# Who writes the causal mask of the scores: TensorE by identity products, or ScalarE by a copy into the score banks

## The chip, the cores and the metric

One Trainium2 chip, one of its cores. The metric is device time in microseconds for one execution of the whole program, lower is better. In the engine names below PE is TensorE (PEld its weight loads), DVE is VectorE, ACT is ScalarE, POOL is GpSimd, SP the engine that only issues transfers here.

## The reference: one decoder layer on 16 sequences of 128 tokens

Three residual blocks, each behind a layer norm: an RWKV-like attention with a decay matrix, a causal attention to a context, and a mixture of 8 experts plus a shared one. The change touches the second block alone:

```python
qp = q @ Wq.T
kv = latent_kv @ Wkv_expand.T
k, v = jnp.split(kv, 2, axis=-1)
...
scores = jnp.einsum('bhqd,bhkd->bhqk', qh, kh) * inv_sqrt_d      # 16 heads of 16
causal = jnp.tril(jnp.ones((sq, sk), dtype=bool))
scores = jnp.where(causal, scores, jnp.finfo(scores.dtype).min)
attn = jax.nn.softmax(scores, axis=-1)
out = jnp.einsum('bhqk,bhkd->bhqd', attn, vh)
```

## The kernel before

**Groups and batches.** The 16 sequences go in four groups of four (`g` = 0 to 3; `GB` = 4 sequences a group, called batches, `b` = 0 to 3). A group passes through the first attention (scores, decay, products), a normalisation and projection stage (points `n0` to `n5`), the causal attention (the x stage, points `x0a` to `x3c`), and the norm, mixed inputs and routing of the third block (`y0`, `r0`, `r1`). The mixture itself, called the feed-forward, of group g-1 is woven into group g in ticks: each engine has its own program, written out by hand in the same order, and at a `point(g, name)` it runs the ticks that stand there. From g = 1 on, a batch of the x stage holds five ticks: two at `a`, one at `b`, two at `c`. The last group's ticks run alone behind it. Order is by program order on each engine and by semaphores between them; there is no scheduler.

**One tick** c of the feed-forward is a chain over all engines: PE `gate_up(c)`, 12 products (L900 to L902), ACT silu (L703), DVE times up (L1301), POOL times the expert's weight (L563, which comes by a transfer `cwb`), ACT copy to `hT` (L697), POOL the rest of `hT` (L557), PE `down(c)`, 6 products (L927 to L929). PE does `gate_up(n)` and `down(n-2)` in one tick. Once a half of the tokens, DVE adds the result to `res` (L1297) before PE may begin the next `down`.

**The x stage of one batch, g >= 1.** Banks 0 to 3 hold the scores of all 16 heads, bank 4 the outputs.
- `query_scores` on PE: for each bank i one product of `identb` with `maskS` (L1091, 512 columns, bf16), which sets the bank to 0 or -1e30; then 8 products of queries and keys onto it (L1098; the profile has each as two passes, so x16).
- `maxima` on DVE: the negated row maxima out of the four banks (L1395, 128x2048), split in two bf16 parts (L1401, L1403). It stands in DVE's order behind `attended` of the batch before (reciprocal L1409, product L1411).
- `turn_maxima` on PE (L1103) and its copy on ACT (L786, `nmT`), then `key_scores` on PE (L1112, L1117): the same scores transposed, with the maxima subtracted.
- `exponentials` on ACT: four activations of 128x512 (L795), each releasing `p_exp`. An exp behind a silu needs a table load (1.28 us), and the silu behind the exps one more.
- POOL cuts the weights to the causal half (L617, four), PE `attend` (L1132, x64) multiplies with the values.

The order on PE is `query_scores(b)`, ticks a, `turn_maxima`, tick b, `key_scores`, ticks c, `attend(b)`, `query_scores(b+1)`. A mask product of batch b+1 waits for `p_exp` of its bank, which has long been there by then. On ACT it is ticks a, `take_maxima`, tick b, `exponentials(b)`, ticks c, ticks a of b+1. In group 0, which has no ticks, two sets of banks take turns; that order is not touched.

Of the kernel before, what the change touches and what calls it, by code (L numbers as in the profile page):

```python
# [10 lines left out]
ACT = mybir.ActivationFunctionType  # L11
AX = mybir.AxisListType.X

P = 128
# [3 lines left out]
def decoder_layer(nc, x, ctx_in, Wr, br, Wk, bk, Wv, bv, Wg, bg, Wo, bo, ln_g, ln_b,  # L18
# [11 lines left out]
    GB = 4  # L30
# [14 lines left out]
    with es:  # L45
        def sb(name, shape, dt):
            return es.enter_context(nc.sbuf_tensor(name, shape, dt))
# [6 lines left out]
        def sem(name):  # L54
            return es.enter_context(nc.semaphore(name))
# [15 lines left out]
        maskS = sb("maskS", [P, P], BF16)  # L71
# [68 lines left out]
        def score_base(g, b):  # L140

            return 4 * (b % 2) if g == 0 else 0

        def weights_of(g, b):

            return pex2 if g == 0 and b % 2 else pex
# [32 lines left out]
        PS = [PSB[:, i, :] for i in range(8)]  # L179
# [72 lines left out]
        q_ready = sem("q_ready")  # L252
        x_scored = sem("x_scored")
        max_ready = sem("max_ready")
        nm_hi = sem("nm_hi")
        nm_ready = sem("nm_ready")
        nm_turned = sem("nm_turned")
# [2 lines left out]
        p_exp = sem("p_exp")  # L260
# [104 lines left out]
        def ticks_at(g, point):  # L365

            count = LAST if g == NG - 1 else COUNT
            first = sum(count[p] for p in POINTS[:POINTS.index(point)])
            return range(first, first + count[point])
# [267 lines left out]
        def _(act):  # L637
# [53 lines left out]
            def ffn_tick(f, n):  # L691
                if 1 <= n <= FN:
                    c = f * FN + n - 1
                    act.wait_ge(h_scaled, c + 1)
                    if c >= 2:
                        act.wait_ge(down_done, c - 1)
                    act.activation(hT[:, c % 2, 0, :], hb[:, c % 2, :], ACT.Copy).then_inc(h_hi, 1)  # L697
                if n < FN:
                    c = f * FN + n
                    act.wait_ge(gu_ready, c + 1)  # L700
                    if c >= 2:
                        act.wait_ge(h_lo, c - 1)
                    act.activation(hb[:, c % 2, :], PS[5 + c % 2][:, 0:HT], ACT.Silu).then_inc(silu_done, 1)  # L703

            def split_high(n):
                act.wait_ge(f_in[n], 32 if n < 4 else 16)
                if n == 4:
                    act.wait_ge(w_tp, 9)
                hi, raw = split_hi(n)
                act.activation(hi, raw, ACT.Copy).then_inc(f_hi, 1)  # L710

            def point(g, name):
                if g:
                    for n in ticks_at(g, name):
                        ffn_tick(g - 1, n)
                else:
                    for n in HIGH_AT.get(name, ()):
                        split_high(n)
# [31 lines left out]
            for g in range(NG):  # L750

                pad_v(g, 0)
                pad_v(g, 1)
                for e in range(3):
                    pad_v(g, 2 * e + 2)
                    pad_v(g, 2 * e + 3)
                    take_y(g, e)
                    if g == 0:
                        split_high(e)
                take_y(g, 3)  # L760

                act.wait_ge(ctx_turned, g + 1)
                act.activation(cT, PS[0][:, 0:HT], ACT.Copy).then_inc(cT_ready, 1)
                point(g, "n0")
                act.wait_ge(kp_ready, g * 4 + 4)
                if g == 0:
                    act.wait_ge(mask_cols, 2)
                for m in range(2):
                    for w in range(2):
                        act.activation(kbd[:, m, w, :].rearrange("p (q e t) -> p e q t", q=2, e=2),  # L770
                                       PSB[:, 1:3, m * HT:(m + 1) * HT].rearrange("p e (q t) -> p e q t", q=2), ACT.Copy,
                                       scale=xcol[:, w:w + 1]).then_inc(kbd_ready, 1)
                point(g, "n1")
                point(g, "n2")
                point(g, "n3")
                point(g, "n4")
                act.wait_ge(xn_turned[1], g * 4 + 4)
                act.activation(xT1[:, 0, :], PS[1][:, :], ACT.Copy).then_inc(xT1_act, 1)
                point(g, "n5")
                for m in range(2):  # L780
                    act.wait_ge(qp_ready, g * 2 + m + 1)
                    act.activation(qT[:, m, :], PS[3 + m][:, :], ACT.Copy, scale=float(XD) ** -0.5).then_inc(q_ready, 1)

                def take_maxima(b):
                    act.wait_ge(nm_turned, g * 4 + b + 1)
                    act.activation(nmT[:], PS[score_base(g, b)].bitcast(BF16)[:, 0:P], ACT.Copy).then_inc(nmT_ready, 1)  # L786

                def exponentials(b, banks):
                    for i in banks:
                        act.wait_ge(t_ready, g * 16 + 4 * b + i + 1)  # L790
                        if i == 0 and b and g:
                            act.wait_ge(o_part, g * 4 + b)
                        elif i == 0 and b >= 2:
                            act.wait_ge(o_part, g * 4 + b - 1)
                        act.activation(weights_of(g, b)[:, i, :], PS[score_base(g, b) + i][:, :], ACT.Exp).then_inc(p_exp, 1)  # L795

                if g == 0:
                    for b in (0, 2):
                        take_maxima(b)
                        exponentials(b, (0, 1))  # L800
                        take_maxima(b + 1)
                        exponentials(b, (2, 3))
                        point(g, f"x{b}a")
                        exponentials(b + 1, range(4))
                        point(g, f"x{b}b")
                else:
                    for b in range(GB):
                        point(g, f"x{b}a")
                        take_maxima(b)
                        point(g, f"x{b}b")  # L810
                        exponentials(b, range(4))
                        point(g, f"x{b}c")

                point(g, "y0")
                if g + 1 < NG:
                    mixed_input(g + 1)
                point(g, "r0")
                point(g, "r1")
                act.wait_ge(xn_turned[2], g * 4 + 4)
                for k in range(2):  # L820
                    act.activation(xTf[:, 0, k, :], PS[k][:, :], ACT.Copy).then_inc(xTf_hi, 1)
                if g + 1 < NG:
                    take_rk(g + 1)
                act.wait_ge(r_step, g * R_STEPS + R_EXP)
                act.activation(r_e[:], r_z[:], ACT.Exp).then_inc(r_exp, 1)
                if g + 1 < NG:
                    take_g(g + 1)
                act.wait_ge(cw_turned, g + 1)
                act.activation(cwT, PS[cw_bank(g)][0:E + 1, :], ACT.Copy).then_inc(cwT_ready, 1)
# [5 lines left out]
        def _(pe):  # L835
# [124 lines left out]
            for g in range(NG):  # L960
# [119 lines left out]
                def query_scores(b):  # L1080
                    t = slice(b * T, (b + 1) * T)
                    for i in range(4):
                        if g == 0 and b >= 2:
                            pe.wait_ge(p_exp, g * 16 + 4 * (b - 2) + i + 1)
                            if i == 0:
                                pe.wait_ge(yT_ready, g * 4 + b - 1)
                        elif g == 0 and b == 1 and i == 0:
                            pe.wait_ge(q_ready, g * 2 + 2)
                        elif g and b:
                            pe.wait_ge(p_exp, g * 16 + 4 * (b - 1) + i + 1)  # L1090
                        mm(PS[score_base(g, b) + i][:, :], identb[:], maskS[:].unsqueeze(1).to_broadcast([P, 4, P]), start=True, stop=False,  # L1091
                           skip_group_check=True)
                        if b == 0 and i == 2:
                            pe.wait_ge(q_ready, g * 2 + 2)
                    for m in range(2):
                        for i in range(4):
                            rows = slice(32 * i, 32 * i + 32)
                            mm(PS[score_base(g, b) + i][:, m * 2 * P:(m + 1) * 2 * P], qT[rows, m, t], kbd[rows, m, :, t], start=False, stop=True,  # L1098
                               skip_group_check=True).then_inc(x_scored, 1)
# [70 lines left out]
                for b in range(GB):  # L1170
                    t = slice(b * T, (b + 1) * T)
# [357 lines left out]
```

## Time and profile before

| | |
|---|---|
| Time, median of 3 runs | 724.67 us (723.44 to 726.44) |
| The profiled execution | 729.72 us, span 728.0 us, mean granted TensorE clock 0.954 |
| Busy: PE, PEld, DVE, ACT, POOL | 645.8, 518.3, 383.1, 270.5, 343.6 us |
| Mask products L1091 | 64 in all, 36 of them in batches 1 to 3 of groups 1 to 3 |
| x stages with ticks | about 218 to 290, 386 to 458, 547 to 620 us |

PE busy is counted by matmul records whose ends are modelled, so that neighbours overlap: four mask products show as 1.04 us, and the next product starts 0.96 us after the first of them. Start times are the better measure on PE.

### The profile page before, as it was taken

Reading aid. Unit: us, or ns where it says so; the run is one execution under the profiler, and the core shown is the slowest. Engines: PE = TensorE matmul, PEld = TensorE weight load, DVE = VectorE, ACT = ScalarE, POOL = GpSimd, SP = SyncE. Lnnn points to the kernel's source line nnn. Section 1 sums busy time; section 2 is a strip of 40 time slices with the busy share of each in tenths; the row PEclk is TensorE's granted clock in tenths of the full one; section 3 lists DMA queues with packets and bytes.
Section 4 is the critical chain, followed back from the end, with each engine's and each line's share of the span. In section 5 each row is a group of like instructions: output and inputs, shape, how many; then the busy total and the mean of one; then the engine's idle time right before and its main releaser. Section 6 shows DMA issues by size and latency. Waiting matters only on the chain.

```text
span 728.0 us, 16212 instructions
## 1 busy us (share of the span) xinstructions
PE 645.8 (89%) x6692; PEld 518.3 (71%) x6692; DVE 383.1 (53%) x781; ACT 270.5 (37%) x591; POOL 343.6 (47%) x470
## 2 busy tenths in 40 slices
PE   6886876788999999898999999898999999759997
PEld 5443355454978789554987788664878889659997
DVE  4887677668534453768542444759543443422221
ACT  4836032222334444232324444231324445213332
POOL 7574244114455555314454555214445555316675
PEclk9989988999999999999899999999999999979999
DMA  8901000020121111011121111002011111012221
GB/s 210 342 5 31 0 2 2 1 57 4 45 73 32 37 56 27 15 34 28 32 75 30 38 53 41 15 1 60 29 46 28 43 53 39 19 30 59 64 77 43
DMA packets 41541, 34.15 MB, mean 47 GB/s; under 512 B 9614, under 2 KB 40919, under 8 KB 41467
## 3 DMA queue, kind: packets, MB, share of 16 engines
q1 hardware_dynamic: 39562, 31.27, 15.4%
q10 hardware_dynamic: 1904, 1.84, 0.8%
q8 instruction: 53, 0.87, 0.5%
q14 instruction: 22, 0.17, 0.1%
HBM read 30.92 MB, written 2.17 MB: 45 GB/s over the span
## 4 chain that ended last, share of the span: by engine, by line
PE 51%; DVE 24%; POOL 12%; issue 5%; ACT 5%; DMA 2%; SPq 1%; POOLq 0%; DVEq 0%; ACTq 0%
DVE A L1326 8%; PE bank L896 5%; PE bank L900 5%; PE bank L901 4%; PE bank L902 4%; PE bank L1060 4%; POOL A L617 4%; PE bank L1132 4%; DVE nm L1395 4%; PE bank L927 4%; POOL hT L557 3%; PE bank L929 3%; PE bank L928 3%; POOL hb L563 2%; PE bank L1077 2%
## 5 line engine op out<-in xcount | busy, mean ns | idle before, releaser
L1301 DVE TENSOR_TENSOR hb<-hb,bank 128x256 f32<-128x256 f32 x136 | 56.9, 419 | 213.3 <-ACT hb L703 213.3
L563 POOL TENSOR_TENSOR hb<-hb,cwb 128x256 f32<-128x256 f32 x136 | 100.4, 738 | 98.7 <-DVE hb L1301 75.1
L557 POOL TENSOR_TENSOR hT<-hb,hT 128x256 fp32r<-128x256 f32 x136 | 101.9, 749 | 74.8 <-ACT hT L697 74.8
L697 ACT ACTIVATE hT<-hb 128x256 fp32r<-128x256 f32 x136 | 57.1, 420 | 174.8 <-POOL hb L563 174.8
L927 PE MATMUL bank<-wDh,hT 128*128 128x256 f32 x272 | 80.2, 295 | 25.7 <-POOL hT L557 20.5
L1326 DVE TENSOR_TENSOR A<-bank,decay 128x512 f32<-128x512 f32 x128 | 77.2, 681 | 19.0 <-PE bank L984 19.0
L900 PE MATMUL bank<-xTf,wGh 128*128 128x256 f32 x272 | 83.3, 306 | 2.1 <-DVE A L1343 2.1
L901 PE MATMUL bank<-xTf,wGh 128*128 128x256 f32 x272 | 77.0, 283 | 0.0
L902 PE MATMUL bank<-xTf,wGl 128*128 128x256 f32 x272 | 76.9, 283 | 0.0
L902 PE MATMUL bank<-xTf,wUl 128*128 128x256 f32 x272 | 76.8, 282 | 0.0
L900 PE MATMUL bank<-xTf,wUh 128*128 128x256 f32 x272 | 76.8, 282 | 0.0
L901 PE MATMUL bank<-xTf,wUh 128*128 128x256 f32 x272 | 76.7, 282 | 0.0
L929 PE MATMUL bank<-wDh,hT 128*128 128x256 f32 x272 | 76.6, 281 | 0.0
L928 PE MATMUL bank<-wDl,hT 128*128 128x256 f32 x272 | 76.5, 281 | 0.0
L519 POOL TENSOR_TENSOR A<-A,mcol 128x512 f32<-128x512 f32 x32 | 33.5, 1053 | 89.5 <-PE bank L984 71.1
L927 PEld LDWEIGHTS bank<-wDh,hT 128*128 128x128 f32 x272 | 52.0, 191 | 31.6 <-POOL hT L557 23.0
L703 ACT ACTIVATE hb<-bank 128x256 f32<-128x256 f32 x136 | 51.2, 377 | 59.4 <-PE bank L902 59.1
L900 PEld LDWEIGHTS bank<-xTf,wGh 128*128 128x128 f32 x272 | 52.2, 192 | 10.7 <-issue 5.0
L900 PEld LDWEIGHTS bank<-xTf,wUh 128*128 128x128 f32 x272 | 52.4, 193 | 0.0
L901 PEld LDWEIGHTS bank<-xTf,wGh 128*128 128x128 f32 x272 | 52.1, 192 | 0.1
L928 PEld LDWEIGHTS bank<-wDl,hT 128*128 128x128 f32 x272 | 52.2, 192 | 0.0
L902 PEld LDWEIGHTS bank<-xTf,wGl 128*128 128x128 f32 x272 | 52.1, 192 | 0.0
(201 smaller groups left out, 1316.7 us busy)
## 6 DMA issues: line engine op xcount, KB each, us to landing
cwb<-cw_rows SPq DMA_DIRECT2D x72, 128.0 KB, 2.9
A<-in_x SPq DMA_DIRECT2D x4, 512.0 KB, 4.7
res<-in_x SPq DMA_DIRECT2D x4, 512.0 KB, 4.2
out_x<-res SPq DMA_DIRECT2D x8, 256.0 KB, 2.6
cwb<-cw_rows SPq DMA_DIRECT2D x16, 112.0 KB, 2.6
cwb<-cw_rows SPq DMA_DIRECT2D x16, 96.0 KB, 2.7
cwb<-cw_rows SPq DMA_DIRECT2D x24, 64.0 KB, 2.6
rawG<-in_L_ffn_w_gate SPq DMA_DIRECT2D x2, 704.0 KB, 7.1
```

The costliest lines, as they stand in the source:

```text
L557: pool.tensor_tensor(hT[:, c % 2, 1, :], hb[:, c % 2, :], hT[:, c % 2, 0, :].bitcast(F32), ALU.subtract).then_inc(h_lo, 1)
L563: pool.tensor_tensor(hb[:, c % 2, :], hb[:, c % 2, :], cwb[:, c % CWS, :], ALU.mult).then_inc(h_scaled, 1)
L697: act.activation(hT[:, c % 2, 0, :], hb[:, c % 2, :], ACT.Copy).then_inc(h_hi, 1)
L703: act.activation(hb[:, c % 2, :], PS[5 + c % 2][:, 0:HT], ACT.Silu).then_inc(silu_done, 1)
L900: mm(out_ap, wh, xh, start=start, stop=False, skip_group_check=skip)
L901: mm(out_ap, wh, xl, start=False, stop=False, skip_group_check=skip)
L902: return mm(out_ap, wl, xh, start=False, stop=stop, skip_group_check=skip)
L927: mm(o, hi[:, t], wDh[:, j, :], start=(j == 0 and b == 0), stop=False, skip_group_check=True)
L928: mm(o, hi[:, t], wDl[:, j, :], start=False, stop=False, skip_group_check=True)
L929: last = mm(o, lo[:, t], wDh[:, j, :], start=False, stop=j == FB - 1, skip_group_check=True)
L1301: tt(hb[:, c % 2, :], hb[:, c % 2, :], PS[5 + c % 2][:, HT:GT], ALU.mult).then_inc(gu_used, 1)
L1326: tt(att[:, (u % 2) * 4 + i, :].rearrange("p (j t) -> p j t", j=4), PS[SCORE_BANKS[(4 * u + i) % 7]][:, :].rearrange("p (j t) -> p j t", j=4),
```

## The change

In groups 1 to 3, for batches 1 to 3, the four mask products are left out on PE. In their place ACT, behind the ticks at `x{b}c` of the batch before, copies `maskS` (bf16, 128x128, read four times over) into each of the banks 0 to 3 (f32, 128x512), and counts up a new semaphore `mask_put`. PE waits for all four counts before the first score product of the batch, and all score products then add onto what ACT wrote. Batch 0 of each group, and all of group 0, keep their products.

```diff
+        mask_put = sem("mask_put")
...
                         point(g, f"x{b}b")
                         exponentials(b, range(4))
                         point(g, f"x{b}c")
+                        if b + 1 < GB:
+                            for i in range(4):
+                                act.wait_ge(p_exp, g * 16 + 4 * b + i + 1)
+                                act.activation(PS[i][:, :].rearrange("p (h t) -> p h t", h=4),
+                                               maskS[:].unsqueeze(1).to_broadcast([P, 4, P]), ACT.Copy).then_inc(mask_put, 1)
...
                         elif g and b:
-                            pe.wait_ge(p_exp, g * 16 + 4 * (b - 1) + i + 1)
+                            pe.wait_ge(mask_put, (g - 1) * 12 + 4 * (b - 1) + i + 1)
+                            continue
                         mm(PS[score_base(g, b) + i][:, :], identb[:], maskS[:].unsqueeze(1).to_broadcast([P, 4, P]), start=True, stop=False,
                            skip_group_check=True)
```

ACT between the exponentials of batch 0 and the ticks of batch 1 in group 1, before the change (`waits` names the semaphores of a row):

```order
L795 ACTIVATE A<-bank 128x512 [waits t_ready] x4
L697 ACTIVATE hT<-hb 128x256 [waits down_done,h_scaled]
L703 ACT_TABLE_LOAD [waits h_lo]
L703 ACTIVATE hb<-bank 128x256 [waits gu_ready]
L697 ACTIVATE hT<-hb 128x256 [waits down_done,h_scaled]
L703 ACTIVATE hb<-bank 128x256 [waits h_lo,gu_ready]
L697 ACTIVATE hT<-hb 128x256 [waits down_done,h_scaled]
L703 ACTIVATE hb<-bank 128x256 [waits h_lo,gu_ready]
```

The same place of the changed kernel, whose lines are one higher here:

```order
L796 ACTIVATE A<-bank 128x512 [waits t_ready] x4
L698 ACTIVATE hT<-hb 128x256 [waits down_done,h_scaled]
L704 ACT_TABLE_LOAD [waits h_lo]
L704 ACTIVATE hb<-bank 128x256 [waits gu_ready]
L698 ACTIVATE hT<-hb 128x256 [waits down_done,h_scaled]
L704 ACTIVATE hb<-bank 128x256 [waits h_lo,gu_ready]
L817 ACTIVATE bank<-maskS 128x512 [waits p_exp] x4
L698 ACTIVATE hT<-hb 128x256 [waits down_done,h_scaled]
```

The four copies stand behind the second silu of `x0c`, ahead of the copy to `hT` of that tick; the table loads stay where they were.

PE at the same place of the program, from the outputs of batch 0 on, before the change:

```order
L1132 MATMUL bank<-A 32x128 [waits p_ready]
L1132 MATMUL bank<-A 32x128 x7
L1132 MATMUL bank<-A,onesp 32x128 x8
L1132 MATMUL bank<-A 32x128 x8
L1132 MATMUL bank<-A,onesp 32x128 x8
L1091 MATMUL bank<-maskS,identb 128x512 [waits p_exp] x4
L1098 MATMUL bank<-A 128x256 x8
L900 MATMUL bank<-xTf,wGh 128x256 [waits gu_used]
```

and with the change, where `attend` is L1139 and the score products L1105:

```order
L1139 MATMUL bank<-A 32x128 [waits p_ready]
L1139 MATMUL bank<-A 32x128 x7
L1139 MATMUL bank<-A,onesp 32x128 x8
L1139 MATMUL bank<-A 32x128 x8
L1139 MATMUL bank<-A,onesp 32x128 x8
L1105 MATMUL bank<-A 128x256 [waits mask_put]
L1105 MATMUL bank<-A 128x256 x7
L906 MATMUL bank<-xTf,wGh 128x256 [waits gu_used]
```

The four wide products are gone, and the first score product has a wait on ACT's fourth copy, with everything behind it on PE.

## Rows read from the trace of the kernel before

**Rows 1.** The page: busy time of the engines, and the chain that ended last.

```profile
PE 645.8 (89%) x6692; PEld 518.3 (71%) x6692; DVE 383.1 (53%) x781; ACT 270.5 (37%) x591; POOL 343.6 (47%) x470
...
PE 51%; DVE 24%; POOL 12%; issue 5%; ACT 5%; DMA 2%; SPq 1%; POOLq 0%; DVEq 0%; ACTq 0%
```

**Rows 2.** Windows (start:end, length, busy by engine, PEclk, DMA): first x stage, and behind it.

```profile
217.90:290.00 72.10, 69.31 (x914) 62.07 (x914) 31.56 (x54) 33.78 (x69) 41.51 (x61) 1.00 0.15 38
...
297.00:300.40 3.40, 2.04 (x13) 1.85 (x14) 1.68 (x4) 0.42 (x1) 1.73 (x3) 0.92 0.00 0
300.40:303.80 3.40, 3.40 (x12) 2.43 (x11) 3.26 (x6) 1.09 (x2) 0.00 (x0) 0.57 0.22 77
```

**Rows 3.** Timeline (start us, length us, engine, line, [idle before]): between batches 1 and 2, group 1.

```profile
251.40 0.37 ACT L703 ACTIVATE hb<-bank 128x256 f32<-128x256 f32 x1
...
252.33 1.04 PE L1091 MATMUL bank<-maskS,identb 128*128 128x512 bf16 x4
...
253.06 0.42 ACT L697 ACTIVATE hT<-hb 128x256 fp32r<-128x256 f32 x1 [1.29 <-POOL hb L563]
253.29 1.15 PE L1098 MATMUL bank<-A 32*128 32x256 f32 x16
...
254.25 0.42 DVE L1411 TENSOR_TENSOR A<-bank,S 128x256 f32<-128x256 f32 x1
254.60 2.28 DVE L1395 TENSOR_REDUCE nm<-bank 128x16 f32<-128x2048 f32 x1
```

**Rows 4.** Timeline: the same pair at batch 0 of group 1, DVE free.

```profile
217.86 1.15 PE L1098 MATMUL bank<-A 32*128 32x256 f32 x16
...
219.15 2.29 DVE L1395 TENSOR_REDUCE nm<-bank 128x16 f32<-128x2048 f32 x1 [5.57 <-PE bank L1098]
```

**Rows 5.** Timeline: from the scores of batch 2 of group 1 to the next outputs.

```profile
261.24 1.28 ACT L795 ACT_TABLE_LOAD   x1
261.29 1.11 PE L1117 MATMUL bank<-A 32*128 32x128 f32 x32
...
262.54 2.07 ACT L795 ACTIVATE A<-bank 128x512 f32<-128x512 f32 x4
...
263.21 2.43 POOL L617 TENSOR_SCALAR_AFFINE_SELECT A<-A 128x512 f32<-128x512 f32 x4 [0.62 <-ACT A L795]
...
265.61 0.72 POOL L557 TENSOR_TENSOR hT<-hb,hT 128x256 fp32r<-128x256 f32 x1
...
266.39 0.39 PE L927 MATMUL bank<-wDh,hT 128*128 128x256 f32 x1 [0.26 <-POOL hT L557]
```

**Rows 6.** Groups of instructions (count, then busy us, mean ns, idle before): prices on ACT.

```profile
L697 ACT ACTIVATE hT<-hb 128x256 fp32r<-128x256 f32 x136 | 57.1, 420 | 174.8 <-POOL hb L563 174.8
...
L795 ACT ACTIVATE A<-bank 128x512 f32<-128x512 f32 x56 | 29.1, 603 | 5.3 <-PE bank L1117 5.0
...
L710 ACT ACTIVATE wGh<-rawG 128x2112 fp32r<-128x2112 f32 x2 | 3.9, 1966 | 0.0
```

**Rows 7.** Timeline: between batches 2 and 3 of group 3, the last of the places.

```profile
596.42 0.37 ACT L703 ACTIVATE hb<-bank 128x256 f32<-128x256 f32 x1
...
598.32 1.15 PE L1098 MATMUL bank<-A 32*128 32x256 f32 x16
```

**Rows 8.** Timeline: between batches 1 and 2 of group 3.

```profile
578.25 0.37 ACT L703 ACTIVATE hb<-bank 128x256 f32<-128x256 f32 x1
...
581.50 1.15 PE L1098 MATMUL bank<-A 32*128 32x256 f32 x16
582.46 0.42 DVE L1411 TENSOR_TENSOR A<-bank,S 128x256 f32<-128x256 f32 x1
...
582.80 2.28 DVE L1395 TENSOR_REDUCE nm<-bank 128x16 f32<-128x2048 f32 x1
```

**Rows 9.** Timeline: PE behind a wait for DVE, batch 1 of group 1.

```profile
243.45 0.38 PE L927 MATMUL bank<-wDh,hT 128*128 128x256 f32 x1 [1.63 <-DVE res L1297]
```

## The prediction

> **What bounds the kernel now.** I read the page's busy shares first, then the chain of work that ended last, then the timeline of all engines around one place where the mask products stand. By busy time PE is far ahead, 89% against 53% for DVE [rows 1], and in the first x stage it is at 69.31 us of 72.1 with the granted clock at 1.00, the 2.4 GHz level [rows 2]. That alone says: take work off PE. But the chain gives PE only 51% of the span, DVE 24% and POOL 12% [rows 1], so I asked what the stage itself waits for.
>
> Between two batches three things meet. PE ends `attend`, starts the mask products at 252.33, and the scores at 253.29, so the four products are worth 0.96 us of PE. DVE starts the maxima at 254.60, which is 1.31 us after the scores start; but it is also the moment at which its own product L1411 (254.25, 0.42 long) lets go [rows 3]. At batch 0, where DVE had been idle for 5.57 us, the lag from scores to maxima is 1.29 us [rows 4]. So at 254.60 both conditions are met within some 0.02 us: the maxima cannot start earlier than DVE's own queue allows, whatever PE saves, and they start later at once if the scores do.
>
> From the maxima the chain has next to no slack. They hold back the feed-forward's DVE step, that holds POOL, then ACT; ACT loads the exp table at 261.24 and starts the exps at 262.54, just as the load ends (262.52), while PE's key scores end at 262.40. POOL's four cuts (263.21, 2.43 long) hold its `hT` step to 265.61, and PE's `down`, ahead of `attend`, is waiting for it until 266.39 [rows 5]. So the chain runs DVE, POOL, ACT, POOL, PE and back, and a later start of the maxima comes out at the next `attend` in full.
>
> **What the change costs, step by step.**
>
> Removed on PE: 9 places x 0.96 us = 8.6 us of PE time [rows 3]. By the paragraph above none of it brings the maxima forward. What hides it is DVE's reciprocal and product; without them the gain would be 0.96 us a place.
>
> Added on ACT: four copies a place, 36 in all, none with a table load, since they stand between a silu and a copy. The trace of before has no activation that writes a bank from the SBUF, so I bound one. An activation from SBUF to SBUF takes 420 ns for 256 columns and 1966 ns for 2112, so (1966 - 420) / 1856 = 0.833 ns a column, and for 512 columns 420 + 256 x 0.833 = 633 ns [rows 6]. Neighbours overlap: four exps from a bank to the SBUF are 603 ns long each [rows 6] and take 2.07 us together, so they start (2.07 - 0.60) / 3 = 0.49 apart [rows 5] and overlap by 0.11. That makes one copy 0.63 us, and 0.52 from start to start. The cheap end is the exps' own price, 0.60 and 0.49. The dear end is 0.63 us each with no overlap at all. I take 0.63 and 0.52, because the source of the copies is the SBUF as in the rows that give them.
>
> Where they stand decides more than their sum. In ACT's order they come behind the second silu of the `c` ticks, and that silu starts at 251.40, only 0.93 us before `attend` ends. The silu is 0.37 long, so with the same overlap the first copy starts 0.26 after it, and the last ends 0.26 + 3 x 0.52 + 0.63 = 2.45 us after the silu's start. PE starts some 0.06 after what releases it (265.61 + 0.72 = 266.33, then 266.39) [rows 5], so the scores start 2.51 after the silu. Before it was 253.29 - 251.40 = 1.89 [rows 3]. The scores are 0.62 us later, and with them the maxima and the whole chain, while PE stands idle for 2.51 - 0.93 = 1.6 us.
>
> How often: the distance from silu to scores is 1.89 to 1.94 at eight of the nine places; the last of the eight is 598.32 - 596.42 = 1.90 [rows 7]. The ninth, between batches 1 and 2 of group 3, has the silu 3.25 us ahead (578.25, 581.50), because PE was held there by the addition to `res`. The copies end at 580.70, the scores start at 580.76, 0.74 earlier than before, but DVE is in its product until 582.88 and the maxima started at 582.80 [rows 8]: no gain, no loss.
>
> Queued behind the copies on ACT: the copy to `hT` of the same tick, 253.06 before [rows 3]. Its place is free only at 251.40 + 0.26 + 4 x 0.52 = 253.7, so it is 0.7 later, and POOL's rest of `hT` with it, to about 255.0. PE needs that only two ticks on, behind 18 and more products, and ACT is then idle until the next silu; nothing waits. Queued behind PE's new wait: the scores and all five ticks. Transfers: none is moved, and SP and POOL pass nothing.
>
> Sum: 8 x 0.62 = 5.0 us, the ninth 0. The profiled execution took 729.72 us (1.7 around its span of 728.0) and would take 734.7; it lies 5.05 us above the median of the runs, which with the same sum gives 724.67 + 5.0 = 729.7. By the cheap copy the last ends at 0.26 + 3 x 0.49 + 0.60 + 0.06 = 2.39, so 0.50 late, 4.0 in all; by the dear one at 0.26 + 4 x 0.63 + 0.06 = 2.84, 0.95 late, 7.6 in all.
>
> A rule to set beside this: ScalarE has a price of 93 ns for its access to the SBUF and 51 ns to a bank, and a bank is its faster destination; so the Trainium skill, "Perfetto Trace Analysis", Optimizing Scalar/DVE Operations, and "ScalarE: Activation LUTs", Step-by-step. By it, an estimate, a copy is 93 + 51 + 427 = 571 ns with 0.52 between starts, the scores start 0.26 + 3 x 0.52 + 0.57 + 0.06 = 2.45 after the silu, and the sum would be 8 x 0.56 = 4.5 us. The trace has no such write, so it can't say yet.
>
> **The rivals.**
> - *The copies are late, by more or less than I price them* (my forecast): 4.0 to 7.6 us slower.
> - *The slack is there after all.* The maxima come 0.62 later, but the exps wait for PE or a table load that I see as tight, or `attend` finds its inputs ready, and part of each 0.62 is absorbed. For: three of the links above are tight only to 0.1 us or so. Against: PE's own ticks shift by the same 0.62, and PE has no gap in which to catch up. With half absorbed it is 8 x 0.31 = 2.5 us, 727.2.
> - *Faster: PE is the bound.* Then the 0.96 us a place counts, 8.6 us in all, 716.0. The point from which it decides: the copies must have ended before `attend` does, that is within 0.93 us of the silu, where the shortest activation of the rows here, 128 columns, already takes 0.27; and the maxima must not wait for L1411. Neither holds in [rows 3]. The Trainium skill says to optimise the engine with the highest occupancy first ("Perfetto Trace Analysis", Identifying the Most-Contended Engine). PE has it here, and that rule would back this rival.
> - *Slower by the clock.* PE will idle 1.6 us at eight places where it now works. The granted clock is 1.00 over the whole x stage, though PE stands idle there once for 1.63 us [rows 9]. Behind the stage it falls to 0.57 in a stretch of 3.4 us, that is for most of it to the 1.2 GHz level, after a stretch in which PE was busy for 2.04 us of 3.4 [rows 2]. At a place of the change PE would be busy for about as little of such a stretch. If a stretch like that followed each of the eight, PE would lose some 1.7 us in it, 14 us on top of 5: 744.
> - *The change doesn't do what it says*: that the accumulation ignores what ACT wrote. It would change values, not the time.
>
> **How the numbers follow.** From no change this kernel can be told by about 0.5%, 3.6 us. Forecast, 728.5 to 733: 0.70, its likeliest 729.7. Slack absorbed, 725 to 728.5: 0.18. Clock falls, 731 for one or two of them to 744 for all: 0.07. Faster: 0.05, partly for falls of the clock elsewhere in the program that shift with the phase. The range of eight in ten goes from 726.5, half the delay absorbed, to 733.5, the dear copy with a microsecond for the clock. The cheap end, 728.7, lies only just beyond 0.5%, so a part of the forecast's own chance goes to no change: slower 0.72 with the clock's, same 0.23, faster 0.05.
>
> **What would show it in the changed profile.** The copies: 36 of them at about 0.6 us, the first 0.26 behind the silu. PE idle 1.5 us before the scores, released by ACT. Scores start 2.5 us after that silu at eight places, maxima 1.3 after the scores. Each x stage longer by about 2 us (1.3 in group 3), the rest as before, PEclk at full grant in the x stages. It would be wrong if the maxima started later but the next `attend` did not, if a copy cost over 0.7 or under 0.45 us from start to start, or if the clock fell.

## The result: 0.8% slower, and what the profile after shows

The changed kernel took 730.36 us, median of 6 runs (728.92 to 734.68), against 724.91 (723.44 to 727.07, 6 runs): ratio 1.0083, 95% interval 1.0054 to 1.0112, some 6 us slower. Timed again beside other kernels it was 1.0113 (1.0073 to 1.0154). The forecast was 729.7 us, slower. One execution of e3_split22 and one of e8_swap fell into a disturbed state of over 1500 us; both are left out, and since the first was the profiled one, e9_split22_look takes its place.

The page of the changed kernel, busy time and chain, to set against [rows 1]:

```profile
PE 638.1 (87%) x6656; PEld 514.0 (70%) x6656; DVE 382.9 (52%) x781; ACT 287.6 (39%) x627; POOL 344.6 (47%) x470
...
PE 41%; DVE 26%; ACT 11%; POOL 11%; issue 7%; DMA 2%; SPq 1%; POOLq 0%; ACTq 0%; DVEq 0%
```

PE has 36 instructions and 7.7 us less, ACT 36 and 17 us more, and in the chain PE fell from 51% to 41% while ACT went from 5% to 11%. The span still grew by 2.6 us. A share of the chain that leaves an engine doesn't mean that time was saved; here most of it went to ACT, which is now waited for. The 2.6 us are less than the timed 6 because single profiles differ outside the x stages as well: e11_before_look2, the unaltered kernel once more, has a span of 720.0 us in place of 728.0, with x stages of the same length.

The place of [rows 3], between batches 1 and 2 of group 1, in the timeline after (here the silu is L704, the maxima L1402, `attend` L1139):

```profile
254.22 0.37 ACT L704 ACTIVATE hb<-bank 128x256 f32<-128x256 f32 x1
...
254.49 2.15 ACT L817 ACTIVATE bank<-maskS 128x512 f32<-128x512 bf16 x4
...
255.16 0.62 PE L1139 MATMUL bank<-A,onesp 128*32 128x128 f32 x16
...
255.85 1.76 DVE L1416 RECIPROCAL S<-bank 128x256 f32<-128x256 f32 x1 [0.80 <-PE bank L1139]
256.57 0.40 ACT L698 ACTIVATE hT<-hb 128x256 fp32r<-128x256 f32 x1
256.78 1.15 PE L1105 MATMUL bank<-A 32*128 32x256 f32 x16 [1.00 <-ACT bank L817]
...
257.64 0.42 DVE L1418 TENSOR_TENSOR A<-bank,S 128x256 f32<-128x256 f32 x1
258.04 2.29 DVE L1402 TENSOR_REDUCE nm<-bank 128x16 f32<-128x2048 f32 x1
```

The first copy starts 0.27 after the silu, the last ends 2.42 after it, and the scores start at 2.56, where before it was 1.89. The maxima start 1.26 behind them. The copy to `hT`, which had started 1.66 after the silu, now stands behind the copies at 2.35. This place lies behind a fall of the granted clock, of which more below: `attend` ends later, so that PE idles only 1.00 us and DVE goes from its product straight into the maxima. The same chain of waits, one batch on and without a fall, with the idle time of PE and DVE ahead of each:

```profile
274.23 1.15 PE L1105 MATMUL bank<-A 32*128 32x256 f32 x16 [1.52 <-ACT bank L817]
...
275.49 2.29 DVE L1402 TENSOR_REDUCE nm<-bank 128x16 f32<-128x2048 f32 x1 [0.50 <-PE bank L1105]
```

Before, DVE went here from its product straight into the maxima, which start 0.08 us ahead of the product's end; now it stands idle for 0.50 us until the scores come. The two together are the 0.6 us by which the step grew. The price of a copy, from the groups of instructions (count, then busy us, mean ns, idle before), and who waited for it (us in all, times, the longest):

```profile
L817 ACT ACTIVATE bank<-maskS 128x512 f32<-128x512 bf16 x36 | 19.3, 590 | 0.0
```

```profile
PE bank L1105 <- ACT bank L817: 11.7, 9, 1.6
```

The ninth place, to set against [rows 8]:

```profile
582.44 0.37 ACT L704 ACTIVATE hb<-bank 128x256 f32<-128x256 f32 x1
...
585.00 1.15 PE L1105 MATMUL bank<-A 32*128 32x256 f32 x16 [0.20 <-ACT bank L817]
...
586.65 0.42 DVE L1418 TENSOR_TENSOR A<-bank,S 128x256 f32<-128x256 f32 x1
586.99 2.28 DVE L1402 TENSOR_REDUCE nm<-bank 128x16 f32<-128x2048 f32 x1
```

The scores start 2.56 after the silu where it was 3.25, so 0.69 earlier, and the maxima don't follow: they start as DVE's product lets go, 1.99 behind the scores.

From maxima to maxima is the measure for the rest of this text, since it is what the chain hands on. Three steps a group, in us, worked out from the starts of L1395 or L1402 in the timelines, an asterisk where the clock's records have a fall inside:

| kernel | group 1 | group 2 | group 3 | sum |
|---|---|---|---|---|
| before | 16.85, 18.60, 16.85 | 16.84, 18.67, 16.86 | 16.84, 18.17, 16.82 | 156.5 |
| changed | 17.45, 19.77*, 17.45 | 17.47, 20.00*, 17.46 | 17.47, 18.18, 17.44 | 162.7 |
| changed, second profile | 17.46, 19.25, 17.45 | 17.45, 20.01*, 17.46 | 17.45, 18.19, 17.44 | 162.2 |

Steps without a fall are 0.60 to 0.65 longer, the one to the ninth place 0.01 to 0.02. Group 1 of the second profile, free of falls, is 54.16 against 52.30, so 1.86 for three places; group 3 is 1.26 for two. With group 2 taken to be like group 1, since no profile has it without a fall, that makes 5.0 us. The rest of the first profile's 6.2, about 1.2 us, are the falls in batch 1, and those had not been in the sum.

### The profile page after: what moved, and what is told of

Read it like the earlier page. It is cut to its first block, busy times and chain, and to the rows that moved or that the text cites. A ratio compares the mean times of both kernels' runs of the same rounds, so it can differ in the third digit from the quotient of the medians.

```text
span 730.6 us, 16194 instructions
## 1 busy us (share of the span) xinstructions
PE 638.1 (87%) x6656; PEld 514.0 (70%) x6656; DVE 382.9 (52%) x781; ACT 287.6 (39%) x627; POOL 344.6 (47%) x470
## 4 chain that ended last, share of the span: by engine, by line
PE 41%; DVE 26%; ACT 11%; POOL 11%; issue 7%; DMA 2%; SPq 1%; POOLq 0%; ACTq 0%; DVEq 0%
DVE A L1333 7%; PE bank L902 5%; DVE nm L1402 5%; POOL hb L564 4%; PE bank L1066 4%; PE bank L906 3%; PE bank L907 3%; PE bank L908 3%; POOL hT L558 3%; PE bank L933 3%; ACT A L796 2%; PE bank L1105 2%; PE bank L1083 2%; ACT bank L817 2%; PE bank L935 2%
## 5 line engine op out<-in xcount | busy, mean ns | idle before, releaser
L704 ACT ACTIVATE hb<-bank 128x256 f32<-128x256 f32 x136 | 51.2, 377 | 55.4 <-PE bank L908 55.2
L902 PE MATMUL bank<-A,wA 128*128 128x512 f32 x96 | 49.0, 657 | 4.4 <-DVE A L1253 2.5
```

The costliest lines, as they stand in the source:

```text
L902: last = mm(bank[:, :], wA[:, i, k, m * P:(m + 1) * P], xm[:, c % 4, :], start=k == 0, stop=k == 1)
```

## The experiments

Twelve runs of nine kernels. Ratios are to the kernel before on the same chip.

**e1_nomask and e2_nomask_swap: what the mask products on PE are worth.** On `before`, with the products left out at the nine places:

```diff
                         elif g and b:
                             pe.wait_ge(p_exp, g * 16 + 4 * (b - 1) + i + 1)
+                            continue
...
-  qT[rows, m, t], kbd[rows, m, :, t], start=False, stop=True,
+  qT[rows, m, t], kbd[rows, m, :, t], start=bool(g and b and m == 0), stop=True,
```

and for the second also DVE's order:

```diff
                         point(g, f"x{b}b")
+                        if b:
+                            attended(b - 1)
                         if b == 2 and g + 1 < NG:
                             layer_apply(0, g + 1, tokx, tokx)
                         point(g, f"x{b}c")
-                        attended(b)
+                    attended(GB - 1)
```

> The kernel before, with the mask products of batches 1 to 3 in groups 1 to 3 left out and nothing in their place; PE still waits for the exps. Left out of the computation: at these nine places the row maxima are taken over all keys and not over the causal ones (POOL's cuts still remove the others from the sums). My theory, that DVE's reciprocal and product hold the maxima and the chain runs through them: the scores start 0.96 us earlier behind attend, the maxima start where they did, the time stays within 1 us of before, ratio 1.000. The rival, PE is the bound: 9 x 0.96 = 8.6 us faster, ratio 0.988.

> As e1_nomask (the same part left out), and on DVE the reciprocal and product of batch b-1 stand behind tick b of batch b and no longer ahead of the maxima of batch b. My theory: now nothing of DVE stands before the maxima, they start 1.3 us after the scores, and the 0.96 us of PE count: 9 x 0.96 = 8.6 us faster than before, ratio 0.988. If another link of the chain (table load, exps, POOL's cuts) holds the next attend: ratio 1.000 again.

Measured: e1_nomask 1.0020 (0.9994 to 1.0046), e2_nomask_swap 0.9865 (0.9815 to 0.9915), 716.44 us. Timeline of e1_nomask at the same place (maxima L1396), then of e2_nomask_swap:

```profile
251.05 0.62 PE L1133 MATMUL bank<-A,onesp 128*32 128x128 f32 x16
...
251.60 1.15 PE L1099 MATMUL bank<-A 32*128 32x256 f32 x16
251.74 1.76 DVE L1410 RECIPROCAL S<-bank 128x256 f32<-128x256 f32 x1 [0.25 <-PE bank L1133]
...
253.53 0.42 DVE L1412 TENSOR_TENSOR A<-bank,S 128x256 f32<-128x256 f32 x1
253.87 2.28 DVE L1396 TENSOR_REDUCE nm<-bank 128x16 f32<-128x2048 f32 x1
```

```profile
249.29 0.62 PE L1133 MATMUL bank<-A,onesp 128*32 128x128 f32 x16
...
249.84 1.15 PE L1099 MATMUL bank<-A 32*128 32x256 f32 x16
...
251.13 2.29 DVE L1396 TENSOR_REDUCE nm<-bank 128x16 f32<-128x2048 f32 x1 [1.40 <-PE bank L1099]
```

In both the scores follow `attend` at once. With DVE's old order the maxima come 2.27 later, as soon as the product lets go, and the first two steps are 16.85 and 18.59, the old ones to 0.01 us: 0.96 us of PE at nine places is worth nothing. With DVE out of the way the maxima come 1.29 later and the first two steps are 15.87 and 17.63, 0.97 to 0.98 shorter; the third is 15.96, 0.89 shorter. The two kernels do the same work and differ only in DVE's order. The mask products cost their full 0.96 us, but only once DVE is not there at the same moment.

**e3_split22 and e9_split22_look: the copies' place.** On the changed kernel:

```diff
-                        point(g, f"x{b}c")
-                        if b + 1 < GB:
-                            for i in range(4):
-                                ...
+                        for k, n in enumerate(ticks_at(g, f"x{b}c")):
+                            ffn_tick(g - 1, n)
+                            if b + 1 < GB:
+                                for i in ((range(2), range(2, 4))[k]):
+                                    ...
```

> The changed kernel, its copies split: two behind the first silu of the c ticks, two behind the second. The same 36 copies on ACT, the same wait on PE, no mask products. My theory, the place of the last copy makes the loss: it ends 0.26 + 0.52 + 0.63 = 1.41 us after the second silu starts, the scores start at 1.47 where before it was 1.89, the maxima are held by DVE as before: time as before, ratio 1.000, 5 us faster than the changed kernel. Rival, the copies cost as work on ACT, or by the clock's falls, wherever they stand: as the changed kernel, ratio 1.007.

> The split of e3_split22 once more, for a profile alone. My theory: the last copy ends 1.4 us behind the second silu, the scores start at 1.5 (0.14 from copy to PE, as the changed kernel showed) where before it was 1.90, and the maxima, held by DVE's product, start 1.7 instead of 1.3 after them, so a batch lasts 16.8 and 18.6 us as before. Rival, work on ACT costs as such: 17.5 and 19.3 us as in the changed kernel.

Measured: 1.0025 (0.9992 to 1.0058), and at a place of group 2 in the second one's timeline:

```profile
418.53 0.37 ACT L704 ACTIVATE hb<-bank 128x256 f32<-128x256 f32 x1
...
418.79 1.11 ACT L818 ACTIVATE bank<-maskS 128x512 f32<-128x512 bf16 x2
...
420.05 1.15 PE L1106 MATMUL bank<-A 32*128 32x256 f32 x16 [0.51 <-ACT bank L818]
...
421.39 0.43 DVE L1419 TENSOR_TENSOR A<-bank,S 128x256 f32<-128x256 f32 x1
421.82 2.29 DVE L1403 TENSOR_REDUCE nm<-bank 128x16 f32<-128x2048 f32 x1
```

The scores start 1.52 after the silu and the maxima wait for DVE; the three steps of this group, which has no fall, are 16.85, 18.71 and 16.86, those of before to 0.05. The same 36 copies with the same wait on PE cost nothing in these steps, and the time of the whole can't be told from that of before. So it is neither the work on ACT nor the wait as such, but where the last copy ends.

**e4_three: one copy less.** Three copies a place, bank 3 masked by a product as before:

```diff
-                            for i in range(4):
+                            for i in range(3):
...
-                            pe.wait_ge(mask_put, (g - 1) * 12 + 4 * (b - 1) + i + 1)
-                            continue
+                            if i < 3:
+                                continue
+                            pe.wait_ge(p_exp, g * 16 + 4 * (b - 1) + i + 1)
...
+                    if g and b:
+                        pe.wait_ge(mask_put, (g - 1) * 9 + 3 * b)
```

> The changed kernel with three copies a place (banks 0 to 2) and one mask product left on PE for bank 3, behind which PE waits for the three copies. My theory: the third copy ends 0.26 + 2 x 0.52 + 0.63 = 1.93 us after the silu, the scores start at 1.99, 0.1 later than before, 0.8 us in all, ratio 1.001. Rival, the loss goes with the ACT work: three quarters of the changed kernel's 5 to 6 us, ratio 1.006.

Measured: 0.9971 (0.9934 to 1.0009). Timeline:

```profile
249.92 0.36 ACT L704 ACTIVATE hb<-bank 128x256 f32<-128x256 f32 x1
...
250.19 1.63 ACT L817 ACTIVATE bank<-maskS 128x512 f32<-128x512 bf16 x3
...
251.87 1.15 PE L1108 MATMUL bank<-A 32*128 32x256 f32 x16 [0.61 <-ACT bank L817]
```

The scores start at 1.95, and the steps are 16.86, 18.66 and 16.86, a sum of 156.7 against 156.5. Three quarters of the copies cost 0.2 us where all four cost 5.0. That is a threshold, not a price for each copy.

**e6_eight: two copies of each bank.** On the changed kernel:

```diff
-                            for i in range(4):
+                            for j in range(8):
+                                i = j % 4
                                 act.wait_ge(p_exp, g * 16 + 4 * b + i + 1)
+                                if j >= 4:
+                                    act.wait_ge(mask_put, (g - 1) * 24 + 8 * b + i + 1)
...
-                            pe.wait_ge(mask_put, (g - 1) * 12 + 4 * (b - 1) + i + 1)
+                            pe.wait_ge(mask_put, (g - 1) * 24 + 8 * (b - 1) + 4 + i + 1)
```

> The changed kernel with every copy made twice, so eight a place and 72 in all, PE waiting for the second of each. With the copies' measured spacing of 0.52 and 0.59 us of length: the last ends 0.27 + 7 x 0.52 + 0.59 = 4.50 us after the silu, the scores start at 4.64, 2.74 later than before at eight places and 4.64 - 3.25 = 1.39 at the ninth. My theory, no link absorbs any of it: 8 x 2.74 + 1.39 = 23.3 us slower than before, ratio 1.032. Rival, there is some slack in the chain or in PE's idle time: less than 20 us, ratio under 1.028.

Measured: 1.0546 (1.0487 to 1.0605), 763.8 us, some 40 us more where I had 23; the maxima's steps sum up to 190.6, 34 us more. The first step of groups 1 and 2 shows the mechanism, with 19.52 and 19.65 for 16.85, 2.7 and 2.8 as worked out. What I had not counted is the clock. Timeline and windows (start:end, length, busy time of PE, PEld, DVE, ACT, POOL, granted clock, DMA) at the second place:

```profile
256.66 4.22 ACT L820 ACTIVATE bank<-maskS 128x512 f32<-128x512 bf16 x8
...
261.02 2.09 PE L1108 MATMUL bank<-A 32*128 32x256 f32 x16 [3.62 <-ACT bank L820]
```

```profile
256.00:259.40 3.40, 1.40 (x52) 1.13 (x44) 2.32 (x3) 3.33 (x8) 1.49 (x3) 1.00 0.17 52
...
261.00:264.40 3.40, 3.38 (x22) 2.66 (x23) 1.17 (x1) 0.22 (x1) 0.73 (x1) 0.50 0.02 5
```

After 3.62 us of idling the granted clock is at 0.50, the 1.2 GHz level, and the score products take 2.09 us where they took 1.15. No link made up for the delay: from the late maxima of batch 1 to the silu ahead of the next copies there are 16.3 us (240.12 to 256.40), where it had been 15.4 (236.00 to 251.40); the added 0.9 falls together with a clock of 0.50 from 239.9 to 243.3. How the 34 us divide into copies and clock was not measured.

**e8_swap and e7_split31_swap: DVE's order alone, and a better version.** e8 is `before` with the DVE edit of e2. e7 is the changed kernel with that edit and `range(3), range(3, 4)` in the edit of e3.

> The kernel before, mask products on PE and all, with only DVE's reciprocal and product moved behind tick b of the next batch. By my theory both conditions of the maxima were met at the same moment, so taking one away leaves the other: maxima 1.3 us after the scores as before, no gain, ratio 1.000 (0.998 to 1.001). If DVE's queue alone had held the maxima, up to 8 us faster.

> The changed kernel with three copies behind the first silu of the c ticks and one behind the second, and with DVE's reciprocal and product of batch b-1 moved behind tick b of batch b. The whole reference is computed. By my theory the single copy ends 0.27 + 0.59 us after the second silu and the scores start at 1.00; that silu is 0.17 later because of the three copies ahead of it. So the scores start at 1.17 by the old count, where before it was 1.90: 0.73 earlier at eight places, 0.98 at the ninth, and the maxima follow 1.3 later: 6.8 us faster than before, ratio 0.991. If DVE's order had not mattered, as e1_nomask against before: 1.000.

Measured: e8_swap 1.0012 (0.9981 to 1.0043), e7_split31_swap 0.9910 (0.9877 to 0.9943), 718.16 us. e7 at the same place:

```profile
252.28 0.37 ACT L704 ACTIVATE hb<-bank 128x256 f32<-128x256 f32 x1
...
252.54 0.60 ACT L818 ACTIVATE bank<-maskS 128x512 f32<-128x512 bf16 x1
...
253.29 1.15 PE L1106 MATMUL bank<-A 32*128 32x256 f32 x16
...
254.55 2.29 DVE L1403 TENSOR_REDUCE nm<-bank 128x16 f32<-128x2048 f32 x1 [1.44 <-PE bank L1106]
```

The steps are 16.04, 17.83 and 16.04, the sum 149.1, 7.4 us less than before; 6.8 had been worked out. Of the kernels that compute the mask as the reference has it, this is the fastest; e2_nomask_swap, with 0.9865 and a sum of 149.0, can't be told from it for certain, and takes its maxima over all keys. A softmax doesn't depend on the number that is subtracted, but a row whose causal scores lie far below that maximum could underflow. In e8 the lag from scores to maxima is 1.29 and the sum 156.6: with the mask products in place, freeing DVE brings nothing, as leaving the products out had brought nothing while DVE stood in the way. Each alone is worth 0, both together some 7.5 us in the steps of e2 and e7, and 6 to 10 us in their times.

**e5_after_again, e10_before_look, e11_before_look2, e12_after_look3: does the new idle time bring the falls of the clock?** The first and last are the changed kernel, the other two the kernel before, without an edit.

> The changed kernel once more, unaltered, timed in five rounds and with a second profile. Its first profile had two falls of the granted clock inside the x stages (at 247 and 415 us), worth 1.3 us, which the profile of before had not. My theory: eight places x 0.65 = 5.1 us lost by the copies' place, whatever the clock does; falls inside the x stages come and go with the execution, since kernels without any copy had them too. Ratio 1.007 to 1.009. Rival, the new idle time of PE brings the falls: both again, in batch 1 of groups 1 and 2.

> The kernel before, a profile alone: how often does the granted clock fall inside its x stages? If a fall there needs the new idle time of the change: none. If it comes with any idle time of PE, as the 1.6 us ahead of L927 in batch 1: one in some executions.

> As e10_before_look, one more execution: none inside the x stages if the falls need the change's idle time, one or two in some executions if not.

> The changed kernel, a third profile: two falls and one fall inside the x stages so far. If the change brings them: one or two again, worth 0.5 to 0.8 us each. The steps without a fall must read 17.5, 19.3 and 17.5 us from scores to scores as before.

The repeated timing gave 1.0113 (1.0073 to 1.0154), above the 1.007 to 1.009 that I had expected. Falls inside the x stages: the changed kernel 2, 1 and 2 in three profiles, the kernel before 0, 2 and 0; e1 and e9 2, e2 1, e4, e7 and e8 none. So they don't need the change. None of the changed kernel's came directly behind the copies, at none of the eight places of its three profiles: each begins some 10 us behind the start of batch 1's scores. They stand in batch 1 behind the wait for the addition to `res`, which both kernels have and in which PE idles about 1.65 us; in the changed kernel's timeline and a window:

```profile
245.74 0.39 PE L933 MATMUL bank<-wDh,hT 128*128 128x256 f32 x1 [1.66 <-DVE res L1304]
...
246.88 1.64 PE L1124 MATMUL bank<-A 32*128 32x128 f32 x32
```

```profile
247.30:250.70 3.40, 3.40 (x38) 3.17 (x31) 0.00 (x0) 2.17 (x5) 2.35 (x4) 0.50 0.14 43
```

and e10_before_look, unaltered:

```profile
409.26 0.38 PE L927 MATMUL bank<-wDh,hT 128*128 128x256 f32 x1 [1.63 <-DVE res L1297]
...
410.38 1.53 PE L1117 MATMUL bank<-A 32*128 32x128 f32 x32
```

The key products take 1.64 and 1.53 us in place of 1.12, and the step is 0.5 to 1.6 us longer. In group 2 of e1_nomask PE came to the same wait 1 us earlier, idled 2.65 us, and the clock was at 0.50 for 6.8 us; that step is 2.3 us longer. So PE time that is saved ahead of this wait can turn into idle time there. The changed kernel had its fall in group 2 in all three profiles, the kernel before in one of three. Three are too few to say that the change makes them more frequent. The nine steps sum up to 156.5, 159.2 and 156.5 us before and to 162.7, 162.2 and 162.8 with the change, on average 5.2 apart, falls included. Outside of them the program took 571.5, 570.2 and 563.5 us before and 567.9, 568.8 and 567.8 with the change: no difference, but a spread of 8 us. So it stays open what the timed loss beyond 5.0 us is (6 us in one set of runs, with an interval of 4 to 8; 8 in the other, with 5 to 11).

## Why the prediction was right

- *The maxima can't start earlier than DVE's queue allows.* Right, and shown: e1_nomask saved the 0.96 us and got 0, e2_nomask_swap got it in full.
- *The price of a copy.* 0.63 us and 0.52 apart were forecast, 0.59 and 0.52 measured. The nearest row, SBUF to SBUF, was a little dear, an exp from a bank (0.603) nearly exact. The estimate that I set beside it from the Trainium skill, "Perfetto Trace Analysis", Optimizing Scalar/DVE Operations, was 571 ns with 0.52 between starts; this trace agrees with the 0.52, and its copies are 19 ns longer.
- *The scores 2.51 us after the silu, 0.62 late.* Measured 2.55 to 2.56, 0.65 late. Two small errors met: the copy was 0.04 shorter, but PE started 0.14 after the last copy's end and not 0.06. The lag from scores to maxima then was 1.26 in place of 1.30, so that the maxima were 0.60 to 0.65 late.
- *Eight places, the ninth free.* Right: 18.18 for 18.17 us, with the scores 0.69 earlier and held by DVE.
- *The whole delay comes out again.* Right: behind late maxima the next step is not shorter by anything, in the changed kernel (19.25 for 18.60, its own 0.65 and no less) or in e6_eight with 2.7 us. The rival of the absorbed slack fell.
- *The copy to `hT` 0.7 late, harmless.* 0.69 late; the steps show no price for it, and e3 and e7, with other places for the copies, none either.
- *The clock at full grant in the x stages.* Wrong in two of three groups. I had taken a single profile without a fall as the rule, and a fall was one of my signs of being wrong. The rival expected them at the eight places; they came in batch 1 at an older wait, where the kernel before has them too in one profile of three. The sum had nothing for them. Whether they are why the measured loss, 5.45 us between the medians, lies above the forecast's 5.0 is not shown; the interval, 4 to 8 us, holds both.

The faster rival, "PE is the bound", is the reading that the busy shares give, and that the rule of the Trainium skill, "Perfetto Trace Analysis", Identifying the Most-Contended Engine, to start with the engine of highest occupancy would give. The trace didn't agree: PE was at 89%, its weight loads at 71% were ahead of the other engines too, and taking 8.6 us of products from it changed nothing that the times can tell (1.0020, 0.9994 to 1.0046).

## What to carry to other kernels

Where work is moved to an engine that idles, its cost is set by the moment at which that engine gets to it in its own order. Here 17 us of work on an idle ACT cost 5 us in one block and nothing with half of each block two instructions earlier. Where two conditions of a step are met at the same moment, relieving either alone brings nothing; look in the timeline for both, and change them together. Before an engine at 89% is relieved, ask what starts at the moment at which it would be done earlier.

## What the runs showed of the hardware

- A copy by ACT from the SBUF (bf16, 128 columns read four times) into a bank, 128x512 f32, takes 590 ns and 0.52 us from start to start; PE starts 0.14 us after the last one's end, where it started 0.06 after POOL's step [rows 5].
- PE idle for 2.3 to 3.6 us ahead of the scores went with the 1.2 GHz level, a granted clock of 0.50, at all nine places of e6_eight. Idle for 1.0 to 1.6 us ahead of the scores, it was followed directly by a fall at none of the eight places in three profiles of the changed kernel. Idle for 1.65 us in batch 1, it was followed by a fall in some executions and not in others of the same kernel.
